# Narrow attention of a perceiver kernel: one exponential for two chunks of keys, and two PSUM banks for the row maxima

## What is computed

```python
q, k, v = split(queries @ Wq), split(ctx @ Wk), split(ctx @ Wv)      # 16 heads of 16 columns
scores = einsum('bhqd,bhkd->bhqk', q, k) / sqrt(16)
scores = where(arange(4096) < valid_lens, scores, NEG)
out = einsum('bhqk,bhkd->bqhd', softmax(scores), v) @ Wo             # 4 batches, 256 queries, 4096 keys
```

## Time and profile before

| | us |
|---|---|
| median of 3 runs | 5173.62 |
| lowest, highest | 5170.07, 5174.48 |
| the profiled execution's own time | 5178.27 |
| its span | 5176.5 |
| mean granted TensorE clock | 0.926 of full |

### The profile page before, as it was taken

How to read it: one execution, slowest core, us unless ns; L and a number is a source line. 1 busy time by engine, 2 the same in 40 slices (tenths; PEclk the granted TensorE clock), 3 DMA queues, 4 the chain that set the end, 5 groups by cost and what they waited for, 6 DMA issues and landing times. The chain is left out here.

```text
span 5176.5 us, 84100 instructions
## 1 busy us (share of the span) xinstructions
PE 4630.7 (89%) x29076; PEld 3228.5 (62%) x29076; DVE 2944.4 (57%) x4530; ACT 2339.4 (45%) x4145; POOL 1589.6 (31%) x1228
## 2 busy tenths in 40 slices
PE   3899999999999999997769999689999999879499
PEld 2566666666666666665458888555555555446366
DVE  4565555655555565554544444356666677545566
ACT  2455555555555555552422222235555556534111
POOL 2365555565555565552013322110000000000000
PEclk8899999999999999998779999889999999955599
DMA  5644444444444444331111111264444432100011
GB/s 200 230 162 158 139 163 152 155 159 156 163 155 162 161 148 141 138 128 44 29 52 49 36 49 37 91 221 145 132 145 144 130 88 63 39 9 1 8 37 41
DMA packets 222737, 577.07 MB, mean 111 GB/s; under 512 B 42796, under 2 KB 130348, under 8 KB 171948
## 3 DMA queue, kind: packets, MB, share of 16 engines
q1 hardware_dynamic: 220480, 566.34, 33.0%
q0 software_dynamic: 1920, 6.29, 0.3%
HBM read 483.15 MB, written 89.39 MB: 111 GB/s over the span
## 5 line engine op out<-in xcount | busy, mean ns | idle before, releaser
L792 POOL TENSOR_TENSOR wa_acc<-wa_acc,wa_probs 128x512 f32<-128x512 f32 x930 | 1215.6, 1307 | 559.4 <-ACT wa_probs L623 507.0
L677 DVE TENSOR_REDUCE wa_mx<-wa_ps_m 128x2 f32<-128x1024 f32 x512 | 626.7, 1224 | 572.0 <-PE wa_ps_m L494 568.5
L623 ACT ACTIVATE wa_probs<-wa_ps_s 128x512 f32<-128x512 f32 x1024 | 557.8, 595 | 604.4 <-PE wa_ps_s L437 550.6
L1316 DVE TENSOR_REDUCE na_mx<-na_ps_m 128x1 f32<-128x512 f32 x1024 | 639.4, 682 | 210.7 <-PE na_ps_m L1153 210.7
L1264 ACT ACTIVATE na_probs<-na_ps_s 128x512 f32<-128x512 f32 x1024 | 550.1, 600 | 406.5 <-PE na_ps_s L1168 401.2
L436 PE MATMUL wa_ps_s<-wa_qh,wa_keys 128*128 128x256 f32 x2048 | 564.4, 307 | 38.9 <-ACT wa_probs L623 35.6
L448 PE MATMUL wa_ps_o<-wa_probs,wa_values 128*64 128x256 f32 x4096 | 558.1, 394 | 0.0
L437 PE MATMUL wa_ps_s<-wa_ql,wa_keys_one 128*128 128x256 f32 x2048 | 518.4, 285 | 0.0
L436 PEld LDWEIGHTS wa_ps_s<-wa_qh,wa_keys 128*128 128x128 f32 x2048 | 394.5, 193 | 163.7 <-issue 84.8
L462 PE MATMUL wa_ps_k<-wa_ctx,wa_w_k 128*128 128x512 f32 x1536 | 414.1, 406 | 52.0 <-DMA wa_ctx<-ctx_split 52.0
L1153 PE MATMUL na_ps_m<-na_keys,na_q 98*128 98x512 f32 x1024 | 420.3, 419 | 30.2 <-DVE na_mx L1316 16.1
(11 more groups left out here) (287 smaller groups left out, 7087.5 us busy)
## 6 DMA issues: line engine op xcount, KB each, us to landing
wa_ctx<-ctx_split SPq DMA_DIRECT2D x256, 1024.0 KB, 5.0
na_ctx<-ctx_split SPq DMA_DIRECT2D x56, 1024.0 KB, 6.8
na_keys<-k_rows SPq DMA_DIRECT2D x192, 256.0 KB
ctx_split<-wa_stage SPq DMA_DIRECT2D x32, 1024.0 KB, 3.9
ge_land<-in_w_all SPq DMA_DIRECT2D x54, 512.0 KB, 5.1
wa_land<-in_ctxT SPq DMA_DIRECT2D x32, 512.0 KB, 6.5
k_rows<-na_k_high SPq DMA_DIRECT2D x64, 256.0 KB, 2.5
k_rows<-na_k_low SPq DMA_DIRECT2D x64, 256.0 KB, 2.3
```

Of the source, the lines that this page charges most:

```text
L623: act.activation(probs[:, c % R, :], ps_s[c % 2][:, :], ACT.Exp).then_inc(exp_done, 1)
L677: dve.tensor_reduce(mx[:, half, :, k], ps_m[:, :, :], AX.X, ALU.max).then_inc(m_taken, 1)
L792: pool.tensor_tensor(acc[:, :], acc[:, :], probs[:, c % R, :], ALU.add).then_inc(summed, 1)
L1316: dve.tensor_reduce(mx[:, j, u:u + 1], ps_m[n % RM][:, :], AX.X, ALU.max).then_inc(m_taken, 1)
```

## The change

Scores get two tiles of two banks each. Chunks 2p and 2p + 1 fill the two halves of one tile, and one exponential of 128x1024 reads both and writes two neighbouring places of `probs`. `exp_done` counts pairs of chunks, so the waits on it are halved, and only even chunks wait ahead of their scores matmul. The maxima keep two banks, so each maxima matmul waits for the reduction of two before. The lead-in uses three of the four score banks under a list of their own.

```diff
-    RP, RS, RM = 12, 3, 3
+    RP, RS, RM = 12, 2, 2
...
-        ps_s = [s.ps(f"ps_s{i}", [P, 512]) for i in range(RS)]
+        ps_s = [s.ps(f"ps_s{i}", [P, 2, 512]) for i in range(RS)]
+        first_banks = [ps_s[0][:, 0, :], ps_s[0][:, 1, :], ps_s[1][:, 0, :]]
...
-                pe.wait_ge(exp_done, 1 + max(n + 1 - RS, 0))
-                pe.matmul(ps_s[n % RS][:, :], keys[a % 2][0:ROWS, c * P:(c + 1) * P],
+                if n % 2 == 0:
+                    pe.wait_ge(exp_done, 1 + max(n // 2 + 1 - RS, 0))
+                pe.matmul(ps_s[n // 2 % RS][:, n % 2, :], keys[a % 2][0:ROWS, c * P:(c + 1) * P],
...
-                pe.wait_ge(exp_done, 1 + a * CH + 4 * u + 4)
+                pe.wait_ge(exp_done, 1 + (a * CH + 4 * u + 4) // 2)
...
-                act.activation(probs[:, n % RP, :], ps_s[n % RS][:, :], ACT.Exp).then_inc(exp_done, 1)
+                act.activation(probs[:, n % RP - 1:n % RP + 1, :], ps_s[n // 2 % RS][:, :, :], ACT.Exp).then_inc(exp_done, 1)
...
-                    exponents(a, c)
+                    if c % 2:
+                        exponents(a, c)
```

More of the change, by code:

```diff
@@ L1197, in _ @@
                     pe.wait_ge(masked, 1 + max(2 * (n - 1) + m + 1, 0))
-                    project_keys(n, m, ps_s[m])
+                    project_keys(n, m, first_banks[m])
                 for half in range(2 if n < CG else 0):
                     pe.wait_ge(v_ready, 1 + max(2 * (n - 1) + half + 1, 0))
-                    project_values(n, half, ps_p if half else ps_s[2])
+                    project_values(n, half, ps_p if half else first_banks[2])
                 if n >= 5:
@@ L1275, in _ @@
                 for half in range(2 if n < CG else 0):
-                    take_values(n, half, ps_p if half else ps_s[2])
+                    take_values(n, half, ps_p if half else first_banks[2])
             take_maximum(0)
@@ L1355, in _ @@
             for n in range(FIRST):
-                mask_keys(n, 0, ps_s[0])
-                mask_keys(n, 1, ps_s[1])
+                mask_keys(n, 0, first_banks[0])
+                mask_keys(n, 1, first_banks[1])
                 if n in (1, 3, 5):
```

## The result

| | before | changed |
|---|---|---|
| median, us | 5171.84 (4 runs) | 5353.95 (4 runs) |
| lowest, highest | 5168.14, 5174.48 | 5347.63, 5364.77 |
| profiled execution's span | 5176.5 | 5363.0 |
| mean granted clock | 0.926 | 0.913 |

The ratio is 1.0355, 95% interval 1.0333 to 1.0377: 182 us slower. The forecast had been 5307 with 5265 to 5345, so the sign was right, and the measured time lies 9 us above the range. Of the 186.5 us between the two spans, 11 lie ahead of the narrow attention's first matmul (3354.4 us into the span, against 3343.2), in a part that the diff leaves alone. So what follows is compared inside the loop, or between medians.

What follows compares the result with a forecast made beforehand. TensorE, busy for 89% of the span, was taken as the bound. Walk 114, exponential 1.3 and clock 18 gave +133 us on the profiled 5178.27, so a median of about 5307, range 5265 to 5345.

Steps and rivals of the forecast that it cites:

- The bound, and the wait that grows: TensorE bounds the kernel; its maxima matmuls' idle time behind reductions rises from some 7 us to over 70.
- The walk, +114: Pairs' loop and lead-in: maxima matmuls wait for two banks, .45 us per ordinary group; 66.4 + 41.3 in pairs 1 to 30.
- The exponential, 1.3 us: Merged exponential takes 1.02 us, hidden by maxima waits except in pair 31: .18 in each of seven groups, +1.3.
- the walk's own .03 a group: Without the maxima wait, the merged exponential would start each weighing at 2.11 against 2.08, some 7 us over 240 groups.
- The clock, +18: Longer idle time behind divisions lowers TensorE's clock after .6 of 30: 12 more dips at 1.5 us each.
- Rival 1: Clock falls more than once a pair, also in the first six chunks: 45 us more, about 5350; chance 0.10.
- Rivals 2 and 4: 2: two maxima banks are enough, about 5174, chance 0.03; 4: long exponential takes 1.89 us, about 5415, chance 0.03.
- Rival 3: Scores weight loads behind exponentials, 63.5 us, are real delay that four banks remove: 5111 to some 5150; chance 0.04.

Runs made afterwards that it cites:

- after_fill_both: Changed kernel plus useless matmuls: 7 in the wait behind each division, one ahead of each waiting maxima matmul at chunks 1 and 2; 5287.48 us, ratio 1.0227.
- rm2_rs4: Kernel before with two maxima banks instead of three and four score banks instead of three, exponentials still single; 5333.30 us, ratio 1.0319.

## Why the prediction was wrong

- **The bound, and the wait that grows: right.** TensorE's wait for reductions, 6.6 to 71.0 us, was named, and its place in each group to .04 us. VectorE idles more than before (342.6 us for the maxima matmuls, against 206.0).
- **The walk, +114: right, a little short.** Taken free of the clock, the loop of after_fill_both is 1106.14 - 1001.85 + 9 (the six stretches before) = 113 us longer, 114 with the start of pair 1, against 66.4 + 41.3 = 108. The ordinary group is 3.54, not 3.51; the start .82, not .77; and the merge's .19 in the last pairs is in it.
- **The exponential, 1.3 us: right in size** (1.024 us where 1.02 was taken, 1.2 in pair 31), with .19 at the end of each of the last pairs left out: 3 in all. The rule of the Trainium skill, Perfetto Trace Analysis, section Optimizing Scalar/DVE Operations, that an unsaturated engine's larger operations can hold others up, is borne out, with about 3 us; the walk's own .03 a group doesn't show while maxima waits cover it.
- **The clock, +18: this term failed.** Held up by fillers, the changed kernel is 66 us faster, 68 with the 2 that the fillers cost. Before, the same loss was 6 x 1.5 = 9. So the term was about +60, over three times its size; by the profiled loops alone it is 1169.63 - 1106.14 - 9 = +54. Two steps of it were wrong. The share of divisions followed by a fall was put at .6, with a line through two points giving .49; 24 of 30, .8, was measured, seven of them with a stretch of double length, which the price of 1.5 us didn't allow for. And the pairs' starts were left to a rival with 0.10, "no dip stands in those chunks today, though TensorE waits there as well"; 13 of 30 had one. The maxima matmuls' weight loads at a pair's start, before and then in the changed kernel:

```profile
3719.01 0.19 PEld L1153 LDWEIGHTS na_ps_m<-na_keys,na_q 98*128 98x128 f32 x1 [0.52 <-DVE na_mx L1316]
3719.61 0.19 PEld L1153 LDWEIGHTS na_ps_m<-na_keys,na_q 98*128 98x128 f32 x1 [0.30 <-DVE na_mx L1316]
3720.21 0.19 PEld L1153 LDWEIGHTS na_ps_m<-na_keys,na_q 98*128 98x128 f32 x1 [0.41 <-DVE na_mx L1316]
3720.81 0.19 PEld L1153 LDWEIGHTS na_ps_m<-na_keys,na_q 98*128 98x128 f32 x1 [0.30 <-DVE na_mx L1316]
```

```profile
3934.45 0.19 PEld L1154 LDWEIGHTS na_ps_m<-na_keys,na_q 98*128 98x128 f32 x1 [0.81 <-issue]
3934.99 0.19 PEld L1154 LDWEIGHTS na_ps_m<-na_keys,na_q 98*128 98x128 f32 x1 [0.35 <-DVE na_mx L1319]
3935.74 0.19 PEld L1154 LDWEIGHTS na_ps_m<-na_keys,na_q 98*128 98x128 f32 x1 [0.45 <-DVE na_mx L1319]
3936.33 0.19 PEld L1154 LDWEIGHTS na_ps_m<-na_keys,na_q 98*128 98x128 f32 x1 [0.41 <-DVE na_mx L1319]
3937.01 0.19 PEld L1154 LDWEIGHTS na_ps_m<-na_keys,na_q 98*128 98x128 f32 x1 [0.38 <-DVE na_mx L1319]
```

On the matmuls' own row that is .19 us of idle time in a start before and .55 now, .40 of it ahead of the first of these five. Forecast 133, with +42 for the clock and +7 for walk and merge, is 182. By the two profiles it is +36 for the clock, and the 11 us ahead of the narrow attention make up the rest of the 186.5.
- **Rivals.** Rival 1 is what happened, in part: 13 more falls at the starts, not 30; its sign, more than 20 stretches at the lower clock, is met with 37. Rivals 2 and 4 fall by the group of 3.54 us and by the 1.024 us. Rival 3 falls by rm2_rs4, where a fourth score bank leaves a pair at 38.35 us: the 62.1 us of loads behind exponentials are still in the changed kernel's profile, and were no delay.

Why a fall lasts longer in some places, and why it comes behind one division or start and not behind another, wasn't tried.

## What to carry to other kernels

Count a buffer's cycle, not an engine's busy share: writing .40 to .50, reading .68 and .11 of handing over make 1.2 to 1.3 us from one write of a bank to the next. Where writes come .47 apart, two banks leave only .94 and three leave 1.41, so a third bank decides although the reader is idle for a third of the time. Price each wait twice, once as time and once as what it does to TensorE's clock, and in a matmul stream find out the second part by filling the wait with useless matmuls. When a wait is to be hidden, look at which instruction waits first in the queue: moving a later one behind other work gives nothing.

## What the runs showed of the hardware that was not expected

- Waits of .35 to .45 us at five maxima matmuls, strung together over some 3 us at a pair's start (.55 us of idle time in all on the matmuls' own row), were followed by a fall of TensorE's clock from 2.4 to 1.2 GHz in 13 of 30 pairs (granted clock 0.60 in the stretch from 3532 to 3536); with a filler ahead of each of the maxima of chunks 1 and 2 in none.
- Matmuls whose result is thrown away made the kernel 66 us faster, 1.2%, by keeping the granted clock at 1.00.
- An exponential that reads two PSUM banks costs 1.024 us, as against 600 ns for one, and saves ScalarE only about 27 us of busy time over 512 of them (523.6 against 550.1 us in the loop).
